# Three bias buffers and one two-row bias matmul in the two mixture layers of a four-layer graph network

## The reference, cut to what matters

```
g * (act(x @ W1[e] + b1[e]) @ W2[e] + b2[e])
```

## Time and profile before

| | us |
|---|---|
| median of 3 runs | 4878.02 |
| lowest and highest run | 4864.59, 4878.45 |
| the profiled execution | 4864.15 |
| its span in the trace | 4862.2 |
| PE busy in it | 4533.4 |
| mean granted clock of PE, as a share of full speed | 0.97 |

### The profile page before, as it was taken

The page is one execution under the profiler, slowest core; times in us unless marked ns, Lnnn a source line. Parts: engine busy times, 40 slices in busy tenths (PEclk is TensorE's granted clock), DMA queues, the critical chain, the costliest instruction groups (busy, mean ns, idle before and its releaser), DMA issues.

```text
span 4862.2 us, 38764 instructions
## 1 busy us (share of the span) xinstructions
PE 4533.4 (93%) x15508; PEld 2064.9 (42%) x15526; DVE 967.5 (20%) x1809; ACT 971.6 (20%) x1797; POOL 88.7 (2%) x168
## 2 busy tenths in 40 slices
PE   8999999999879998999999999977699999999998
PEld 6544444444424544444444444433344433333343
DVE  3672111212201234212300000012523000000000
ACT  0121112323203325322210101011621111100100
POOL 1000000000000000000000000000000000000000
PEclk9999999999989998999999999988799999999999
DMA  9403222121361120112203030264024999999998
GB/s 323 135 15 129 66 68 82 61 65 61 120 259 60 46 74 18 39 39 100 74 27 103 26 104 26 82 231 172 1 65 185 420 412 423 412 423 411 417 416 355
DMA packets 128785, 795.70 MB, mean 164 GB/s; under 512 B 13950, under 2 KB 26542, under 8 KB 82172
## 3 DMA queue, kind: packets, MB, share of 16 engines
q1 hardware_dynamic: 116892, 728.07, 39.7%
q0 software_dynamic: 9280, 45.81, 2.6%
q10 hardware_dynamic: 2464, 19.67, 1.0%
HBM read 774.47 MB, written 56.83 MB: 171 GB/s over the span
## 4 chain that ended last, share of the span: by engine, by line
PE 85%; DMA 6%; DVE 4%; ACT 3%; issue 1%; SPq 0%; POOL 0%; ACTq 0%; DVEq 0%; POOLq 0%
PE bank L518 76%; DMA mem<-in_experts 4%; PE bank L680 4%; PE bank L516 2%; PE bank L647 2%; DMA mem<-moe_up 1%; DVE rstd L1982 1%; DVE mem L2287 1%; DVE mem L2283 0%; ACT mem L1669 0%; ACT mem L1824 0%; ACT mem L1690 0%; DMA by_slot<-mem,slot_i 0%; ACT mem L1349 0%; DVE mem L1985 0%
## 5 line engine op out<-in xcount | busy, mean ns | idle before, releaser
L518 PE MATMUL bank<-mem 128*128 128x512 f32 (+5 forms) x11160 | 3558.0, 563 | 76.7 <-DMA mem<-in_experts 25.1
L518 PEld LDWEIGHTS bank<-mem 128*128 128x128 f32 (+3 forms) x11160 | 1490.7, 169 | 2075.7 <-issue 1935.8
L518 PE MATMUL bank<-mem,ones 128*128 128x512 f32 (+2 forms) x630 | 247.5, 605 | 104.4 <-DMA mem<-moe_up 61.4
L516 PE MATMUL bank<-ident,mem 128*128 128x128 f32 (+1 forms) x1492 | 223.0, 301 | 77.3 <-DMA mem<-by_slot 11.6
L516 PEld LDWEIGHTS bank<-ident,mem 128*128 128x128 f32 (+1 forms) x1492 | 185.7, 155 | 176.7 <-issue 94.1
L1349 ACT ACTIVATE mem<-bank 128x512 f32<-128x512 f32 x168 | 99.7, 597 | 546.0 <-PE bank L518 541.4
L1349 ACT ACTIVATE mem<-bank,cols 128x512 f32<-128x512 f32 (+1 forms) x91 | 62.4, 686 | 731.2 <-PE bank L518 731.2
L518 PEld LDWEIGHTS bank<-mem,ones 128*128 128x128 f32 (+2 forms) x630 | 90.3, 176 | 236.3 <-issue 184.0
L680 PE MATMUL bank<-mem 128*128 128x512 bf16 x798 | 178.3, 382 | 1.2 <-DVE mem L2068 0.3
L2553 DVE TENSOR_TENSOR mem<-mem,EV 128x512 f32<-128x512 f32 x48 | 33.2, 692 | 552.5 <-ACT EV L1919 552.5
L2531 DVE TENSOR_TENSOR mem<-mem,bank 128x512 f32<-128x512 f32 x48 | 33.0, 687 | 459.1 <-PE bank L518 459.1
(11 more groups left out here) (333 smaller groups left out, 1973.7 us busy)
## 6 DMA issues: line engine op xcount, KB each, us to landing
mem<-in_experts SPq DMA_DIRECT2D x282, 1536.0 KB, 12.1
mem<-in_weights SPq DMA_DIRECT2D x329, 512.0 KB, 3.5
mem<-moe_up SPq DMA_DIRECT2D x30, 1152.0 KB, 6.0
mem<-moe_down SPq DMA_DIRECT2D x30, 1152.0 KB, 8.4
moe_up<-in_weights SPq DMA_DIRECT2D x16, 1152.0 KB
moe_down<-in_weights SPq DMA_DIRECT2D x16, 1152.0 KB
mem<-in_weights POOLq DMA_DIRECT2D x36, 384.0 KB, 7.6
mem<-in_experts ACTq DMA_DIRECT2D x6, 1536.0 KB, 14.9
```

Of the source, the lines that this page charges most:

```text
L516: ins = nc.tensor.transpose(out, lhsT, ident[0:lhsT.shape[0], 0:lhsT.shape[0]])
L518: ins = nc.tensor.matmul(out, lhsT, rhs, start=start, stop=stop)
```

## The change

Three things. The bias rows of a set's two experts lie in two partitions of one buffer, and one matmul with a two-row stationary tile (`pair_rows`: row 0 is 1 for output partitions 0 to 63, row 1 for 64 to 127; POOL makes it at the start, out of `ident`, between the two affine_selects) writes the bias of both halves of the bank. There are three bias buffers in place of two, used by p % 3. And SP's wait for the bias buffer stands ahead of the weight load of e=0, and names the end of D(p-3) (from p=3 on) or the last transposes of the normalised tokens (p=2); p=0 and p=1 have none.

```diff
--- before.py
+++ after.py
@@ -189,7 +189,7 @@
         slot_rows = [area(T_, 4, D), area(T_ + 12, 4, D)]
         slot_rows_t = [area(PQ_, KC, P), area(PQ_ + 3, KC, P)]
         moe_hidden_t = [area(F_, 3, P), area(F_ + 1.5, 3, P)]
-        moe_b = [area(F_ + 3, 2, BIAS, rows=1), area(XN_, 2, BIAS, rows=1)]
+        moe_b = [area(kb, 1, BIAS, rows=2)[:, 0, :] for kb in (F_ + 3, F_ + 7.5, XN_)]
         moe_y = [area(A_ + 45, 1, D)[:, 0, :], area(E_ + 9, 1, D)[:, 0, :]]
         logit_rows = area(PQ_ + 6, 1, N, rows=ME)[:, 0, :]
         zeros = area(F_ + 4, 1, D)[:, 0, :]
@@ -227,6 +227,7 @@
         before_me, limits, counted, first_slot, over_slot, over_number = (
             sb("before_me", [P, P]), sb("limits", [P, OVER]), sb("counted", [P, ME, OVER]), sb("first_slot", [P, ME]),
             sb("over_slot", [P, ME]), sb("over_number", [1, OVER]))
+        pair_rows = sb("pair_rows", [2, P])
         over_f, over_i = sb("over_f", [1, 4, OVER]), sb("over_i", [1, 3, OVER], i32)
         slot_i = sb("slot_i", [P, NT], i32)
         bias_rows = sb("bias_rows", [MF * ME // P, 2 * P])
@@ -249,7 +250,7 @@
         onehot_ready, onehot_used = sem("onehot_ready"), sem("onehot_used")
         spilled = [sem(f"spilled{r}") for r in range(REL4 + 1)]
         moe_w_in = [sem(f"moe_w_in{i}") for i in range(6)]
-        moe_b_in, packed = [sem("moe_b_in0"), sem("moe_b_in1")], [sem("packed0"), sem("packed1")]
+        moe_b_in, packed = [sem(f"moe_b_in{i}") for i in range(3)], [sem("packed0"), sem("packed1")]
         rows_out, slots_in = sem("rows_out"), [sem(f"slots_in{i}") for i in range(3)]
         y_out, y_last, y_in = [sem("y_out0"), sem("y_out1")], sem("y_last"), [sem(f"y_in{t}") for t in range(NT)]
         zeros_out, bias_out = sem("zeros_out"), sem("bias_out")
@@ -294,7 +295,7 @@
         def bias_count(moe, p):
 
             each = lambda q: 16 * (rows_of(q) // BLOCK)
-            return (moe == "moe2") * sum(each(q) for q in range(p % 2, SETS, 2)) + sum(each(q) for q in range(p % 2, p + 1, 2))
+            return (moe == "moe2") * sum(each(q) for q in range(p % 3, SETS, 3)) + sum(each(q) for q in range(p % 3, p + 1, 3))
 
         def shared_step(p, u):
 
@@ -358,13 +359,13 @@
                         sp.wait_ge(dve_done.sem, dve_done.at((tag, "over")))
                     source = (moe_up if kind == "up" else moe_down)[n]
                     one = slice(b, b + 1) if b < ME else bass.ds(expert(b), 1)
+                    if kind == "up" and e == 0 and p == 2:
+                        sp.wait_ge(bank_full.sem, bank_full.at((tag, "rows", KC - 1)))
+                    elif kind == "up" and e == 0 and p > 2:
+                        sp.wait_ge(agg_done.sem, agg_done.at((tag, "down", p - 3)))
                     sp.dma_start(moe_w[h % 6], source[one].rearrange("a p w -> (a p) w")).then_inc(moe_w_in[h % 6], 16)
                     if kind == "up":
-                        if p == 1 and e == 0:
-                            sp.wait_ge(bank_full.sem, bank_full.at((tag, "rows", KC - 1)))
-                        elif p >= 2 and e == 0:
-                            sp.wait_ge(agg_done.sem, agg_done.at((tag, "down", p - 2)))
-                        sp.dma_start(moe_b[p % 2][:, e, :], moe_bias[n][one]).then_inc(moe_b_in[p % 2], 16)
+                        sp.dma_start(moe_b[p % 3][e:e + 1, :], moe_bias[n][one]).then_inc(moe_b_in[p % 3], 16)
 
             sp.wait_ge(feat_in[3], 16)
             moe_pack(0, MOE_AT["moe0"])
@@ -415,6 +416,10 @@
             nc.gpsimd.affine_select(out=ident[:, :], in_=ident[:, :], compare_op=ALU.not_equal, fill=1.0,
                                                    base=0, pattern=[[-1, P]], channel_multiplier=1).then_inc(
                                                            pool_done.sem, pool_done.tick("consts"))
+            pool.wait_ge(pool_done.sem, pool_done.at("consts"))
+            nc.gpsimd.tensor_copy(pair_rows[:, :].rearrange("p (e r) -> p e r", e=2),
+                                  ident[0:2, 0:2].rearrange("p (e a) -> p e a", a=1).to_broadcast([2, 2, BLOCK])).then_inc(
+                                      pool_done.sem, pool_done.tick("pair_rows"))
             nc.gpsimd.affine_select(out=before_me[:, :], in_=before_me[:, :], compare_op=ALU.is_gt, fill=0.0,
                                     base=0, pattern=[[1, P]], channel_multiplier=-1).then_inc(
                                         pool_done.sem, pool_done.tick("before_me"))
@@ -823,11 +828,10 @@
                 def up(p):
                     own = half_rows[:rows_of(p) // BLOCK]
                     w = [weights("up", 2 * p + e) for e in range(len(own))]
-                    pe.wait_ge(moe_b_in[p % 2], bias_count(tag, p))
+                    pe.wait_ge(moe_b_in[p % 3], bias_count(tag, p))
                     if p >= 2:
                         pe.wait_ge(act_done.sem, act_done.at((tag, "act", p - 2)))
-                    for e, r in enumerate(own):
-                        mm(bank[4 + p % 2][r, 0:MF], ones[0:1, 0:BLOCK], moe_b[p % 2][:, e, 0:MF], True, False)
+                    mm(bank[4 + p % 2][0:rows_of(p), 0:MF], pair_rows[0:len(own), 0:rows_of(p)], moe_b[p % 3][0:len(own), 0:MF], True, False)
                     pe.wait_ge(bank_free.sem, bank_free.at((tag, "slots_t", p, 1)))
                     for k in range(KC):
                         for e, r in enumerate(own):
@@ -849,8 +853,8 @@
                     for half in range(2):
                         if p:
                             pe.wait_ge(dve_done.sem, dve_done.at((tag, "y", p - 1, half)))
-                        for e, r in enumerate(own):
-                            mm(bank[6 + half][r, 0:MF], ones[0:1, 0:BLOCK], moe_b[p % 2][:, e, MF + half * MF:MF + (half + 1) * MF], True, False)
+                        mm(bank[6 + half][0:rows_of(p), 0:MF], pair_rows[0:len(own), 0:rows_of(p)],
+                           moe_b[p % 3][0:len(own), MF + half * MF:MF + (half + 1) * MF], True, False)
                         pe.wait_ge(bank_free.sem, bank_free.at((tag, "hidden_t", p)))
                         for f in range(3):
                             for e, r in enumerate(own):
```

## The result

| | before | after |
|---|---|---|
| median of the runs, us | 4877.67 (4 runs) | 4754.04 (4 runs) |
| lowest and highest | 4864.59, 4878.45 | 4747.26, 4761.39 |
| span of the profiled execution | 4862.2 | 4759.6 |
| mean granted clock | 0.970 | 0.976 |
| first layer, first load to the end of D7 | 193.5 | 138.6 |

The changed kernel takes 0.9756 of the time of the one before (95% interval 0.9739 to 0.9773), 2.4% less. The last three lines are from the traces: a layer's stretch runs from SP's first load of up weights to the end of D7. In the changed kernel these are 1270.32 to 1408.90 us and 3128.33 to 3260.28 us.

What follows compares the result with a forecast made beforehand. PE's own work was taken as the bound, except for stalls on late up weights in the mixture layers. Gains 54.8 + 55.5 + 2.8 + 3.8 = 116.9 us off 4864.15 gave 4747; plus half of 13.9, 4754 us, range 4730 to 4786.

Steps and rivals of the forecast that it cites:

- the step from the profile to the median: Whole kernel: half of the 13.9 us between profiled run and median added to 4747, giving 4754 us.
- Part 1: Mixture layers: moving the bias-buffer wait ends PE's stalls ahead of U2 to U6; gain 54.8 and 55.5 us.
- The walk through the list: Mixture layers' loads followed step by step: every load lands 2 to 4 us ahead of its use, no stall left.
- Part 2: Layer start: first loads issued some 20 us earlier, ahead of the scatter, shorten its last piece; gain 2.8 and 3.8 us.
- A gather of the same rows takes 4.39: Last scatter piece: a gather's 4.39 us taken as its time without loads, against 7.16 and 8.14 us.
- I take 0: U0 at each layer's start: no gain counted from a kept clock; bounds 0 and 3.2 us a layer.
- Part 3: Mixture layers: merging removes 42 bias matmuls; gain taken as 0, bounds a gain of 6 us and a loss of 20.
- Counting records: Bias matmuls: the tempting estimate of 42 x 0.35 us off, which the prediction rejected.
- (a): Mixture layers: DMA engines become the bound, 13.8 us a set, 15 us a layer lost; 4784 us, chance 24%.
- (b): More gain than counted: U0 keeps its clock (6 us), merged matmul gains 6; 4742 us, inside the forecast's 72%.
- (c): Mixture layers: the stall only moves to another wait for D(p-2); 4864 us, chance 3%.
- (d): Slower: array drains and idles at each of 42 merged matmuls, 3.5 us a place; 4901 us, chance 1%.

Runs made afterwards that it cites:

- early first loads: matmul alone with the second bias buffer outside the tokens' area and no bias-buffer wait for p=1; 4860.74 us, ratio 0.9970.
- numbers read first: Changed kernel with SP reading both expert numbers of an overflow pair ahead of its buffer wait; 4754.26 us, ratio 0.9739 to before.
- the fillers: Kernel before, with six filler matmuls of 512 columns on PE ahead of each of U2 to U6; 4861.75 us, ratio 0.9961.
- bias behind weights: Kernel before, two buffers, but SP issues both up weight halves ahead of the bias-buffer wait and the bias rows behind it; 4833.74 us, ratio 0.9902.
- matmul alone: Kernel before with only the merged bias matmul added, two bias buffers and the old waits; 4875.92 us, ratio 0.9995.
- Late first loads: Changed kernel with a wait for the tokens' last transposes put ahead of all of U1's loads; 4776.83 us, ratio 0.9783 to before.
- wait alone: Changed kernel without the merged matmul: three bias buffers and moved wait, one-row bias matmuls as before; 4750.53 us, ratio 0.9737 to before.
- changed, again: The changed kernel run once more with the same code; 4754.81 us, ratio 0.9743 to before.

## Why the prediction was right, and where it was not

The time was forecast at 4754 us and measured at 4754.04. The mechanism held, but that the number agrees so well is luck: three terms were off by 4.9, 7.5 and 1.7 us and cancel to 0.9, and the step from the profile to the median added 7 us for no reason. Point by point:

**Part 1, the wait.** Forecast 110.3 us. From early first loads to the changed kernel the layers fall from 376.0 to 270.6, that is 105.4 us; this comparison holds the bias matmul and the first loads fixed. (By the changed kernel's second execution it would be 100.2.) Right in mechanism: waits for moe_up gone, SP's wait at the bias load gone, U2 to U6 at 4.9 us with clock 1.00, 11.8 us a set at the start. The term mis-sized is the transfer: I took the 433 GB/s of one window of 2 us, and let every load land 2 to 4 us ahead. In the first layer the engines moved 405 to 413 GB/s over whole sets, the lead was used up at U4, a set took 12.6 us from there, and 3.0 and 0.4 us of waits came back in the two layers. The walk through the list also put SP's reads of the expert numbers at nothing, without a reason; the share of 0.80 ahead of U4 and the waits of 0.4 us with the numbers read first show that they have a part in it. That half clock is a part of a stall's price was shown by the fillers. That the weights behind the wait, and not the row alone, were what came late was shown by bias behind weights.

**Part 2, the early loads.** Forecast 6.6 us, and 0 for U0's clock. Measured 14.1 us (matmul alone against early first loads). Late first loads, with 19.7 us, delays all of U1, more than the change moved, and is an upper bound. Two steps failed. "A gather of the same rows takes 4.39": the scatter with no loads beside it takes 3.04, which gives 4.1 and 5.1 us in place of 2.8 and 3.8. And "I take 0" for the clock ahead of U0: it kept its upper level in the second layer of the changed kernel (U0 4.86 us for 7.97), and in the first less of U0 was slow than before (6.55 us for 7.49), after the same 1.2 us of idleness. The bounds were there, 0 and 3.2 us; the value chosen was the wrong end in one of two layers.

**Part 3, the bias matmuls.** Forecast 0, from bounds of a gain of 6 us and a loss of 20. Over both layers it lost 0.5 us (changed kernel against wait alone) and 1.7 us (matmul alone against before), both below what two executions of one kernel differ by. The single pieces say the same more surely: 0.84 us against 0.79 from start to start, D 5.85 against 5.78 us, U1 4.86 against 4.83; 0.05 us at each of 42 places is an estimate of 2 us lost. Counting records would have said 15 us. This is the one term in which the number of instructions misleads most, and the row of the last set, with one expert, gave it away. Why two records of full width take 0.84 us and not 0.65 isn't shown; a change between widths on both sides is a guess that fits.

**The sum.** 105.4 + 14.1 - 1.7 = 117.8 us; forecast 116.9. The three are differences of one kernel to the next, so they add up to 388.4 - 270.6 by construction.

**The step from profile to median.** I added 7 us, half of the 13.9 between the profiled execution and the median, without a reason. The table shows where the 13.9 come from: the rest of the span was 4473.8 us in that one execution, and 4478 to 4493 in the twelve others. The profiled execution before was the odd one: the 35 runs of this kernel beside the experiments took 4867 to 4886 us, and none was as short. In the stretch after the first layer, where ACT and DVE share the work with PE, a window of 100 us from 1863 us had a granted clock of 0.90 before; the like window from 1811 us had 0.77 after. To take the gain off the median, as would have been sound, gives 4878 - 117 = 4761, the upper end of what was measured. So the 7 us hit by luck. Of the measured gain of 123.6 us the layers of the two traces give 118. Where the other 6 lie is not shown; the second comparison of the two kernels, 5 runs against 9, has 123.0 (its interval 118 to 132), which speaks against chance alone. The range, 4730 to 4786, is a little wider than its own terms, which give 4735 and 4784.

**The rivals.** (a) was half true: in the first layer the DMA engines were busy throughout from U4 on, but at 12.6 us a set and not 13.8, and the waits of both layers came to 3.4 us, where (a) asked for 30 with the clock. In changed, again they came to 5.0 us, with 3.3 us of half clock behind one of them. By the limit of about 358 GB/s that the Trainium skill gives for loads from HBM (DMA: Bandwidth & Descriptors, Where 436 GB/s comes from) a set would have taken an estimated 14.3 us. The traces disagree: the windows of a set's length in which the engines were busy throughout show 405 to 424 GB/s. (b) came true in one layer of two for U0's clock, and not for the matmul. (c) and (d) are not seen; the ratio of matmul alone, 0.9995 with an upper end of 1.0005, leaves at most 2.4 us for (d), within its 95%.

## What to carry to other kernels

SP issues in order, and so the wait for a 4.5 KB buffer became a wait for the 1152 KB loads behind it, 34 us a layer: look at what stands behind a wait, not only at what it protects, and give the small buffer the same depth as the weights whose loads follow it. Price a standstill with the slow clock behind it, and count matmuls by the time from start to start, since those on two halves of the array ran side by side. When the bound is gone, ask at once for the next one with the rate over a whole set, not that of the best window.

## What the runs showed of the hardware that was not expected

- Behind a short idle time the length of it doesn't say whether the clock falls. After 1.0 us of waiting it stayed at 1.00. Ahead of U0 PE stood idle 1.15 to 1.38 us in 14 layers of the traces with early first loads; U0 was fast in 8 of them (4.86 us after 1.23 and after 1.38) and slow in 6 (6.55 us after 1.19, 6.50 after 1.34). After 1.66 us in one execution U4 took 8.24 us, and after 1.9 and 2.0 us U2 and U3 took 6.5 us; but 1.91 us ahead of U7 of the kernel before (1437.92 to 1439.83) cost nothing: U7 takes 4.84 us in the earlier trace rows.
- A scatter of 128 rows of 3 KB to HBM lands 3.04 us after its issue with no loads beside it, 7.0 to 8.1 us beside 3.5 MB of loads, 9.7 to 10.0 beside 4.7 MB. The gather takes 4.1 to 4.6 us.
- With all but the same code, the part of the span outside the two layers differed between executions by up to 19 us. Most of it stands between the layers: 1703 us in the kernel before, 1715 in matmul alone, 1719 in the changed kernel. Where it was looked at it went with the clock (0.90 against 0.77 in the like windows above).
